# Wavelet attention in an eight-phase layer: the value products cut into four pieces, the result stored in five

## The chip, the cores and the metric

The kernel runs on one core of a Trainium2 chip. The metric is the device time of one execution in microseconds (us); lower is better. A core has five engines that run their own instruction streams and meet at semaphores: TensorE (PE in the profile, with its weight loads as PEld), VectorE (DVE), ScalarE (ACT), GpSimd (POOL) and SyncE (SP), which here only issues transfers (DMA).

## The reference

The input is `hidden_states`, 2 sequences of 2048 tokens with 128 channels, in f32. The kernel computes a chain of residual layers: a state-space (Mamba) block with a tanh block, a wavelet attention, a mixture of 8 experts, a sparse attention layer (4 of 16 heads), a layer with the diagonal of a softmax, and the sparse attention layer again. The change touches the wavelet attention and the end of the last layer. Cut to the wavelet attention and the last step:

```
xe, xo = x[:, 0::2], x[:, 1::2]
a, det = (xe + xo) * inv, (xe - xo) * inv          # 2 x 1024 x 128
q, k, v = (a @ w).reshape(B, 1024, 16, 8)           # 16 heads of 8 channels
att = softmax(einsum('bqhd,bkhd->bhqk', q, k) / sqrt(8))
o = einsum('bhqk,bkhd->bqhd', att, v) @ wo
...
return x + sparse_attention(layernorm(x))           # the last layer; its sum is the result
```

## The kernel before

The kernel is written engine by engine, with explicit semaphores. Each phase has one Python list of steps, and each engine walks it and emits its own part of every step, so the list sets the order on all engines. A `Signal` counts events; `T.wait_ge(*signal(event))` makes TensorE wait for one.

The wavelet attention is `phase_C`. It works in 8 rounds: 2 sequences times 4 groups of 4 heads. A round has 8 blocks of keys (`kt`, 128 keys each), and a block has 4 steps (`hh`, one head each), so 32 steps. The text calls these steps 0 to 31. A step is:

- E: `pe_exp` (L1432), two bf16 matmuls of 512 queries each, scores with the keys on the partitions, into a slot of two PSUM banks; ScalarE then takes the exponential of all 1024 (L1704) into one of the 8 buffers of `prob`.
- M: `pe_max` (L1420), two bf16 matmuls of the scores of the next round, queries on the partitions; VectorE reduces them to a row maximum (L1563). Steps 3, 10, 17 and 24 hold two of these, so that all 32 are made in steps 0 to 27. The last round has none.
- AV: `pe_av` (L1443), the product of the probabilities of the block before with the values (8 channels and a column of ones for the denominator). One call makes one half (512 queries) for 4 heads: f32 matmuls at `tile_position=(0, 32 * hh)`, so that the four heads share the array side by side. Each f32 matmul is two records in the profile, so a half is 8. The result accumulates in PSUM banks 6 and 7 over the 8 blocks of the round.

M and E share 3 PSUM slots in turn (`pe_slot`): a matmul waits until the user three places ahead of it has been read, by ScalarE after an E and by VectorE after an M. The halves of AV stand in front of E at `hh` 2 and 3 of the next block; the two halves of the last block stand in the step `fin` behind the round, after a wait for the last exponential. VectorE then copies banks 6 and 7 out (L1582). ScalarE waits, at the first head of a block, for the second half of the products that last read its buffer.

Two rounds carry more VectorE work than the others: the first has a layer norm beside it, the fifth (sequence 1, group 0) the convolution of sequence 0. The last round has transposes and routing for the next phase beside it.

The last layer is `phase_E("E2")`. Each tile of 128 tokens gets its last addition into `res` from L2480, which raises `summed` (`out_added`). After the phase `finish` waits for the drains of all engines (`enter(SP)`) and then stores all of `res` in one DMA of 2 MB.

Of the kernel before, what the change touches and what calls it, by code (L numbers as in the profile page):

```python
# [11 lines left out]
P = 128  # L12
D = 128
BANK = 512
# [85 lines left out]
def build(nc, a, out, shape, phases=("M", "C", "D", "E", "F", "E2")):  # L100
    NB, S, _ = shape
    NT = S // P
    R = NB * NT
    T, V, A, G, SP = nc.tensor, nc.vector, nc.scalar, nc.gpsimd, nc.sync
    ctx = ExitStack()
    with ctx:
# [1074 lines left out]
            return fd  # L1181

        routers = []

        def phase_C():
            routers.append(front_D())
# [5 lines left out]
            MR = NG * HD  # L1192
            INV = 0.7071067811865476
            SC = 1.0 / float(np.sqrt(HD))
            with ExitStack() as st:
                wqkv = sb(st, "w_qkv", [P, 3 * D])
                wo = sb(st, "w_o", [P, D])
# [110 lines left out]
                second_pass = signal("wl_shifted", at("exp"))  # L1308
                exped = signal("exp_done", at("exp"))
                quads = [(b, g, kt) for b, g in rounds_c for kt in range(CT)]  # L1310
                valued = signal("valued", [(*q, j) for q in quads for j in range(2)])
                oc_done = signal("out_copied", rounds_c)
                o_turned = signal("out_turned", pair("norm", 2))
                o_done = signal("wl_o_done", pair("norm", 2))
# [109 lines left out]
                def pe_exp(b, g, kt, hh):  # L1424
                    n = round_at[b, g]
                    if kt == 0:
                        T.wait_ge(*q_again(n, hh))
                    if kt and hh in (2, 3):
                        pe_av(b, g, kt - 1, hh - 2)
                    bk = pe_slot("exp", b, g, kt, hh)  # L1430
                    for j in range(2):
                        last = T.matmul(bank(bk + j), kT[n % 3][0:ROWS, hh, kt * P:(kt + 1) * P], qT[n % 3][0:ROWS, hh, j * BANK:(j + 1) * BANK], start=True, stop=True)  # L1432
                    last.then_inc(*second_pass.up(b, g, kt, hh))

                def pe_av(b, g, kt, j):

                    if j == 0:
                        T.wait_ge(*exped(b, g, kt, 3))
                        if kt == 0 and round_at[b, g]:
                            T.wait_ge(*oc_done(*rounds_c[round_at[b, g] - 1]))  # L1440
                    for hh in range(4):
                        n = unit_at[b, g, kt, hh] % 8
                        last = T.matmul(bank(6 + j)[32 * hh:32 * hh + HD + 1, :], vp[b][:, kt, 4 * g + hh, :],  # L1443
                                        prob[:, n, j * BANK:(j + 1) * BANK], start=(kt == 0), stop=(kt == CT - 1),
                                        skip_group_check=True, tile_position=(0, 32 * hh))
                    last.then_inc(*valued.up(b, g, kt, j))

# [31 lines left out]
                def pe():  # L1479
                    enter(T)  # L1480
                    for kind, *u in seq:
                        if kind == "turn":
                            pe_turn(*u)
                        elif kind == "qkv":
                            pe_qkv(*u)
                        elif kind == "max":
                            pe_max(*u)
                        elif kind == "exp":
                            pe_exp(*u)
                        elif kind == "fin":  # L1490
                            for half in range(2):
                                pe_av(*u, CT - 1, half)
                        elif kind == "norm":
                            pe_norm(*u)
                        elif kind == "co":
                            pe_co(*u)
                        elif kind == "wo":
                            pe_wo(*u)
                        elif kind == "yt":
                            pe_yt(*u)  # L1500
                        elif kind == "dch":
                            pe_dch(*u)
                        elif kind == "dlg":
                            fd.pe_logits(0, pe_slot("dlg"))
                        elif kind == "dgt":
                            fd.pe_gates(0, pe_slot("dgt"))
                    leave(T)
# [68 lines left out]
                    last.then_inc(*max_rows.up(b, g))  # L1576

                def dve_fin(b, g):
                    V.wait_ge(*valued(b, g, CT - 1, 1))
                    if round_at[b, g]:  # L1580
                        V.wait_ge(*o_turned(*rounds_c[round_at[b, g] - 1], 1))
                    V.tensor_copy(oc[:, :], two(6)).then_inc(*oc_done.up(b, g))  # L1582
# [116 lines left out]
                def act_exp(*u):  # L1699
                    A.wait_ge(*second_pass(*u))  # L1700
                    n = unit_at[u]
                    if n >= 8 and n % 4 == 0:
                        A.wait_ge(*valued(*quads[n // 4 - 2], 1))
                    A.activation(prob[:, n % 8, :], two(slot("exp", *u)), ACT.Exp, scale=SC).then_inc(*exped.up(*u))  # L1704

                def act():
# [491 lines left out]
        def phase_E(tag):  # L2198
# [4 lines left out]
            with ExitStack() as st:  # L2203
# [103 lines left out]
                def sp():  # L2307
                    enter(SP)
                    for b in range(NB):
# [2 lines left out]
                            fr.sp_heads(b)  # L2312
                        sp_swap(2 * b)
                    sp_swap(3)
                    leave(SP)

                def pe_piece(n, m, bk):
# [682 lines left out]
                pool()  # L3000

        def finish():
            enter(SP)
            store = loads("store")
            SP.dma_start(out.rearrange("b (i p) d -> p (b i) d", p=P), res[:, :, :]).then_inc(*store.one())
            SP.wait_ge(*store.all())

        run = {"M": phase_M, "C": phase_C, "D": phase_D, "E": lambda: phase_E("E"), "E2": lambda: phase_E("E2"), "F": phase_F}
# [24 lines left out]
```

## Time and profile before

| | us |
|---|---|
| three timed runs | 4373.02, 4373.57, 4366.19; median 4373.02 |
| profiled execution | 4358.43 |
| its span | 4357.1 |
| PE busy, share of the span | 3635.9 (83%) |
| DVE busy | 3294.0 (76%) |
| ACT busy | 2845.8 (65%) |
| POOL busy | 1001.8 (23%) |
| TensorE granted clock, mean | 0.823 |

The phases run one after the other; the wavelet rounds lie between about 636 and 1100 us from the span's start. In the chain that ended last, followed over the whole span, PE takes 41%, DVE 29%, "issue" 12% and ACT 6%. A record of a matmul lasts longer than the time after which the next can start, because matmuls are pipelined: the distance between the starts of two neighbours is what one costs. Each row of the timeline is start, duration, engine, line, operation, output and inputs, shape, count, and in brackets how long the engine was idle before it and who released it.

### The profile page before, as it was taken

The page shows a single profiled execution, that of the slowest core. Times are in us where ns is not written, and L with a number is a line of the kernel's source. Part 1 is how long each engine was busy: PE and PEld are TensorE (multiplying, and loading weights), DVE is VectorE, ACT ScalarE, POOL GpSimd, SP SyncE. Part 2 cuts the span into 40 slices and gives each one's busy share as a digit, 9 for nine tenths or more (in the row PEclk, how much of TensorE's full clock was granted, in tenths as well). Part 3 has the DMA queues.
Part 4 walks back from the last instruction along what each step waited for, and adds up shares of the span by engine and source line. Part 5 has one row for each costly group of instructions (what it writes and reads, how often), then busy time and mean ns, then how long its engine had stood idle before and what let it go on. Part 6 is the DMA issues. An engine that isn't in the chain of part 4 may idle for free.

```text
span 4357.1 us, 74462 instructions
## 1 busy us (share of the span) xinstructions
PE 3635.9 (83%) x28950; PEld 1917.7 (44%) x28950; DVE 3294.0 (76%) x5091; ACT 2845.8 (65%) x4856; POOL 1001.8 (23%) x1479
## 2 busy tenths in 40 slices
PE   6999868999799998999997666666666659899998
PEld 4666522222344445666665112222222215566776
DVE  6787767777311127887886999999999996778887
ACT  3655415556344445666664999999999995566665
POOL 2444432100467640000001232322332220000000
PEclk8999959999999999999998555555555559899999
DMA  1000032331511200000000111111110110000000
GB/s 48 1 1 1 1 69 38 54 58 20 114 26 37 39 17 9 12 7 12 2 2 16 22 22 22 22 22 22 22 19 19 22 20 21 7 12 7 7 2 21
DMA packets 256813, 97.51 MB, mean 22 GB/s; under 512 B 223795, under 2 KB 241854, under 8 KB 256446
## 3 DMA queue, kind: packets, MB, share of 16 engines
q1 hardware_dynamic: 256462, 92.74, 10.8%
q8 instruction: 231, 3.78, 0.4%
q14 instruction: 120, 0.98, 0.1%
HBM read 31.75 MB, written 2.23 MB: 8 GB/s over the span
## 4 chain that ended last, share of the span: by engine, by line
PE 41%; DVE 29%; issue 12%; ACT 6%; DMA 1%; POOL 0%; SPq 0%; DVEq 0%; ACTq 0%; POOLq 0%
DVE d_negmax L2825 14%; PE psum L2351 7%; PE psum L2380 6%; DVE f_m_E L2450 6%; PE psum L2366 6%; PE psum L2055 5%; PE psum L2077 5%; ACT d_junk L2883 3%; DVE wl_negmax L1563 3%; PE psum L1443 2%; PE psum L1432 2%; DVE f_pT_E L2469 2%; PE psum L1420 2%; ACT wl_p L1704 1%; DVE residual L2480 1%
## 5 line engine op out<-in xcount | busy, mean ns | idle before, releaser
L2825 DVE TENSOR_REDUCE d_negmax<-psum 128x1 f32<-128x1024 f32 x1024 | 1170.9, 1210 | 25.4 <-PE psum L2761 23.4
L2883 ACT ACTIVATE d_junk<-psum,d_negmax 128x1024 bf16<-128x1024 f32 x1024 | 1136.0, 1125 | 37.1 <-DVE d_negmax L2825 32.6
L2761 PE MATMUL psum<-d_qT,d_kT 64*128 64x512 bf16 x2048 | 622.9, 604 | 432.1 <-ACT d_junk L2883 414.9
L2544 ACT ACTIVATE hidden<-psum,f_nm_E 128x1024 f32<-128x1024 f32 x512 | 566.0, 1112 | 143.5 <-DVE f_nm_E L2453 143.4
L2450 DVE TENSOR_REDUCE f_m_E<-psum 128x1 f32<-128x1024 f32 x512 | 601.6, 1216 | 46.8 <-PE psum L2351 45.6
L2351 PE MATMUL psum<-f_k_E,f_q_swapped_E 64*128 64x512 f32 x1024 | 526.9, 624 | 6.6 <-ACT hidden L2544 6.6
L2351 PE MATMUL psum<-f_k_E,f_q_E 64*128 64x512 f32 x1024 | 526.6, 624 | 2.9 <-DVE f_v_E L2441 1.9
L2551 ACT COPY f_pT_E<-psum 128x512 f32<-128x512 f32 x512 | 299.4, 585 | 322.3 <-PE psum L2366 322.3
L2380 PE MATMUL psum<-f_pT_E,f_v_E 128*64 128x128 f32 x8192 | 505.0, 276 | 2.5 <-DVE residual L2480 2.5
L2761 PEld LDWEIGHTS psum<-d_qT,d_kT 64*128 64x128 bf16 x2048 | 107.9, 101 | 842.9 <-ACT d_junk L2883 761.1
L2469 DVE COPY f_pT_E<-psum 128x512 f32<-128x512 f32 x512 | 351.3, 686 | 159.5 <-PE psum L2366 150.0
L2380 PEld LDWEIGHTS psum<-f_pT_E,f_v_E 128*64 128x64 f32 x8192 | 443.6, 137 | 20.0 <-ACT f_pT_E L2551 2.8
L2366 PEld LDWEIGHTS psum<-ident,hidden 64*128 64x128 f32 x8192 | 317.9, 140 | 238.2 <-issue 189.1
L1704 ACT ACTIVATE wl_p<-psum 128x1024 f32<-128x1024 f32 x256 | 255.4, 1023 | 240.3 <-PE psum L1432 239.0
L2366 PE MATMUL psum<-ident,hidden 64*128 64x64 f32 x8192 | 358.6, 227 | 50.7 <-DVE f_pT_E L2469 47.1
L2189 POOL TENSOR_TENSOR moe_h<-moe_h,moe_gates_on_all 128x512 f32<-128x512 f32 x256 | 322.3, 1291 | 320.9 <-DMA moe_gates_on_all<-moe_gate_spill 187.5
L1563 DVE TENSOR_REDUCE wl_negmax<-psum 128x1 f32<-128x1024 f32 x256 | 303.7, 1219 | 77.7 <-PE psum L1420 74.9
L2167 ACT ACTIVATE moe_h<-psum,moe_b 128x512 f32<-128x512 f32 x256 | 174.8, 687 | 254.7 <-PE psum L2077 254.6
L2055 PE MATMUL psum<-moe_h,moe_w 128*128 128x512 f32 x512 | 231.6, 594 | 1.8 <-POOL moe_h L2189 1.5
L2883 ACT ACTIVATION_READ_ACCUMULATOR d_junk<-psum,d_negmax 128x1 f32 x1024 | 214.4, 209 | 0.0
L2077 PE MATMUL psum<-normed_channels,moe_w 128*128 128x512 f32 x448 | 205.0, 601 | 4.9 <-DMA moe_w<-in_moe_w 4.9
L2351 PEld LDWEIGHTS psum<-f_k_E,f_q_E 64*128 64x128 f32 x1024 | 160.5, 189 | 92.9 <-ACT hidden L2544 79.2
(331 smaller groups left out, 4736.3 us busy)
## 6 DMA issues: line engine op xcount, KB each, us to landing
moe_gates_on_all<-moe_gate_spill SPq DMA_DIRECT2D x16, 1024.0 KB, 11.9
f_q_swapped_E<-f_q_E SPq DMA_DIRECT2D x64, 128.0 KB, 2.3
moe_w<-in_moe_w SPq DMA_DIRECT2D x15, 256.0 KB, 6.5
out<-residual SPq DMA_DIRECT2D x1, 2048.0 KB, 8.7
residual<-in_hidden_states SPq DMA_DIRECT2D x2, 768.0 KB, 7.3
wl_qT<-wl_q_rows SPq DMA_TRANSPOSE x48, 3.3
residual<-in_hidden_states SPq DMA_DIRECT2D x2, 256.0 KB, 3.5
m_taps<-in_m_conv SPq DMA_DIRECT2D x4, 128.0 KB
```

Source lines behind the costliest of these rows:

```text
L1563: V.tensor_reduce(negm[:, i, h:h + 1], two(slot("max", b, h, i)), X, ALU.max, negate=True).then_inc(*maxed.up(b, h, i))
L2055: last = T.matmul(acc, w2[:, e * FT + f, :], hbuf[:, n % 2, f, :], start=False, stop=(e == E_ - 1 and f == FT - 1))
L2077: T.matmul(bank(f), w1(e)[:, f * P:(f + 1) * P], chans[:, b, PAD + g * BANK:PAD + (g + 1) * BANK], start=True, stop=True).then_inc(*made.u ...
L2351: last = T.matmul(bank(2 * f + jj), (q if jj == h else q_sw)[half, w, qs], k2[half, w, h, f, :], start=True, stop=True)
L2366: last = T.transpose(bank(4 + r)[:, q * 64:(q + 1) * 64], pb[half, u % 2, kt * P:(kt + 1) * P], ident[half, half])
L2380: last = T.matmul(bank(6)[64 * h:64 * h + 64, 0:P], vt[:, n % 2, kt, h, :], pT[:, (2 * t + h) % 4, kt, :], start=(kt == 0), stop=(kt == NT ...
L2450: last = V.tensor_reduce(m2[:, u % 4, f:f + 1], two(2 * f), X, ALU.max)
L2469: V.tensor_copy(pT[:, u % 4, 8 * g:8 * g + 8, 64:P], bank(5).rearrange("p (q n) -> p q n", n=64)).then_inc(*pT_dve.up(u, g))
L2544: A.activation(pb[:, u % 2, f * 2 * BANK:(f + 1) * 2 * BANK], two(2 * f), ACT.Exp, bias=nm[:, u % 4:u % 4 + 1], scale=SC, accum_out=rs[:, ...
L2761: last = T.matmul(bank(2 + 2 * (at % 3) + jj), kT[half, s, jb * P:(jb + 1) * P], qT[half, s, hf * BANK:(hf + 1) * BANK], start=True, stop= ...
L2825: V.tensor_reduce(mh[:, t % 2, n // 2, n % 2:n % 2 + 1], two(2 + 2 * (at % 3)), X, ALU.max, negate=True).then_inc(*maxed.up(at))
L2883: A.activation(junk[:, at % 3, :], two(2 + 2 * (at % 3)), ACT.Exp, bias=mh[:, t % 2, n // 2, n % 2:n % 2 + 1], accum_out=sh[:, t % 2, n // ...
```

## The change

Two parts. In `phase_C`, an AV call now makes a quarter (256 queries, `AV = 4` pieces of a block), and one piece stands in front of each E: pieces 0 to 2 of the block before at `hh` 1 to 3, and piece 3 of the block before that at `hh` 0. `fin` has five pieces, the last of block 6 and the four of block 7. The waits for `valued` name the last piece. At the end, the one store in `finish` becomes five, issued by SP inside `E2`, each behind the addition of its last tile: 16 tiles (all of sequence 0), 8, 4, 3 and 1.

```diff
+            AV = 4
...
-                    if kt and hh in (2, 3):
-                        pe_av(b, g, kt - 1, hh - 2)
+                    if hh and kt:
+                        pe_av(b, g, kt - 1, hh - 1)
+                    if hh == 0 and kt >= 2:
+                        pe_av(b, g, kt - 2, AV - 1)
                     bk = pe_slot("exp", b, g, kt, hh)
...
+                    size = 2 * BANK // AV
+                    at = j * size % BANK
                     for hh in range(4):
                         n = unit_at[b, g, kt, hh] % 8
-                        last = T.matmul(bank(6 + j)[32 * hh:32 * hh + HD + 1, :], vp[b][:, kt, 4 * g + hh, :],
-                                        prob[:, n, j * BANK:(j + 1) * BANK], start=(kt == 0), stop=(kt == CT - 1),
+                        last = T.matmul(bank(6 + j * size // BANK)[32 * hh:32 * hh + HD + 1, at:at + size], vp[b][:, kt, 4 * g + hh, :],
+                                        prob[:, n, j * size:(j + 1) * size], start=(kt == 0 and at == 0), stop=(kt == CT - 1),
                                         skip_group_check=True, tile_position=(0, 32 * hh))
...
-                            for half in range(2):
-                                pe_av(*u, CT - 1, half)
+                            pe_av(*u, CT - 2, AV - 1)
+                            for j in range(AV):
+                                pe_av(*u, CT - 1, j)
...
-                        A.wait_ge(*valued(*quads[n // 4 - 2], 1))
+                        A.wait_ge(*valued(*quads[n // 4 - 2], AV - 1))
...
+        stored = [(0, NT), (NT, NT + NT // 2), (NT + NT // 2, R - 4), (R - 4, R - 1), (R - 1, R)]
...
+                    if tag == "E2":
+                        for lo, hi in stored:
+                            b, i = (hi - 1) // NT, (hi - 1) % NT
+                            SP.wait_ge(*summed(((b * NPAIR + NPAIR - 1) * NT + i), 1))
+                            SP.dma_start(out_rows[:, lo:hi, :], res[:, lo:hi, :]).then_inc(*store.one())
...
         def finish():
-            enter(SP)
-            store = loads("store")
-            SP.dma_start(out.rearrange("b (i p) d -> p (b i) d", p=P), res[:, :, :]).then_inc(*store.one())
             SP.wait_ge(*store.all())
```

On TensorE, the fourth round (sequence 0, group 3), steps 18 to 21, before. L1443 is AV, L1432 is E, L1420 is M; x4 counts the matmuls of the program, one a head.

```order
L1443 MATMUL psum<-wl_p,wl_v 9x512 x4
L1432 MATMUL psum<-wl_qT,wl_kT 128x512 x2
L1420 MATMUL psum<-wl_kT,wl_qT 128x512 x2
L1443 MATMUL psum<-wl_p,wl_v 9x512 x4
L1432 MATMUL psum<-wl_qT,wl_kT 128x512 x2
L1420 MATMUL psum<-wl_kT,wl_qT 128x512 x2
L1432 MATMUL psum<-wl_qT,wl_kT 128x512 x2
L1420 MATMUL psum<-wl_kT,wl_qT 128x512 x2
L1432 MATMUL psum<-wl_qT,wl_kT 128x512 x2
L1420 MATMUL psum<-wl_kT,wl_qT 128x512 x2
L1443 MATMUL psum<-wl_p,wl_v 9x512 x4
```

The same steps in the changed kernel, where AV is L1451, E is L1438 and M is L1424.

```order
L1451 MATMUL psum<-wl_p,wl_v 9x256 x4
L1438 MATMUL psum<-wl_qT,wl_kT 128x512 x2
L1424 MATMUL psum<-wl_kT,wl_qT 128x512 x2
L1451 MATMUL psum<-wl_p,wl_v 9x256 x4
L1438 MATMUL psum<-wl_qT,wl_kT 128x512 x2
L1424 MATMUL psum<-wl_kT,wl_qT 128x512 x2
L1451 MATMUL psum<-wl_p,wl_v 9x256 x4
L1438 MATMUL psum<-wl_qT,wl_kT 128x512 x2
L1424 MATMUL psum<-wl_kT,wl_qT 128x512 x2
L1451 MATMUL psum<-wl_p,wl_v 9x256 x4
L1438 MATMUL psum<-wl_qT,wl_kT 128x512 x2
L1424 MATMUL psum<-wl_kT,wl_qT 128x512 x2
```

Two halves in front of two of the four E have become four quarters, one in front of each.

On TensorE, the end of the same round before, from the last M to the first E of the next round:

```order
L1420 MATMUL psum<-wl_kT,wl_qT 128x512 x2
L1432 MATMUL psum<-wl_qT,wl_kT 128x512 x4
L1443 MATMUL psum<-wl_p,wl_v 9x512 x4
L1432 MATMUL psum<-wl_qT,wl_kT 128x512 x2
L1443 MATMUL psum<-wl_p,wl_v 9x512 x4
L1432 MATMUL psum<-wl_qT,wl_kT 128x512 x2
L1443 MATMUL psum<-wl_p,wl_v 9x512 x8
L1432 MATMUL psum<-wl_qT,wl_kT 128x512 x2
```

and in the changed kernel:

```order
L1424 MATMUL psum<-wl_kT,wl_qT 128x512 x2
L1451 MATMUL psum<-wl_p,wl_v 9x256 x4
L1438 MATMUL psum<-wl_qT,wl_kT 128x512 x2
L1451 MATMUL psum<-wl_p,wl_v 9x256 x4
L1438 MATMUL psum<-wl_qT,wl_kT 128x512 x2
L1451 MATMUL psum<-wl_p,wl_v 9x256 x4
L1438 MATMUL psum<-wl_qT,wl_kT 128x512 x2
L1451 MATMUL psum<-wl_p,wl_v 9x256 x4
L1438 MATMUL psum<-wl_qT,wl_kT 128x512 x2
L1451 MATMUL psum<-wl_p,wl_v 9x256 x20
L1438 MATMUL psum<-wl_qT,wl_kT 128x512 x2
```

There is a piece in front of each of the last four E, and 20 matmuls of 256 in place of 8 of 512 behind the last; the first four of the 20 belong to the block before and do not wait for the last exponential.

On SP, the end of the program before, from the last swaps of queries (L2303 and L2304) to the store:

```order
L2303 DMA f_q_swapped_E<-f_q_E 64x512 [waits ffn_qk_done]
L2304 DMA f_q_swapped_E<-f_q_E 64x512
L2303 DMA f_q_swapped_E<-f_q_E 64x512 [waits ffn_qk_done]
L2304 DMA f_q_swapped_E<-f_q_E 64x512
L3005 DMA out<-residual 128x32x128 [waits phase_end_act,phase_end_pool,phase_end_dve,phase_end_pe]
```

and in the changed kernel:

```order
L2312 DMA f_q_swapped_E<-f_q_E 64x512 [waits ffn_qk_done]
L2313 DMA f_q_swapped_E<-f_q_E 64x512
L2328 DMA out<-residual 128x16x128 [waits out_added]
L2328 DMA out<-residual 128x8x128 [waits out_added]
L2328 DMA out<-residual 128x4x128 [waits out_added]
L2328 DMA out<-residual 128x3x128 [waits out_added]
L2328 DMA out<-residual 128x128 [waits out_added]
```

The stores stand behind the last swap and wait for additions, no longer for the drains of the four other engines.

## Rows read from the trace of the kernel before

**Rows 1.** Windows, four wavelet rounds: stretch, busy us, clock, DMA share, GB/s.
```profile
758.94:820.28 61.34, 55.06 (x265) 14.39 (x266) 42.22 (x49) 32.09 (x32) 8.69 (x26) 0.89 0.33 62
820.28:875.82 55.54, 51.01 (x265) 13.27 (x264) 41.94 (x49) 31.99 (x32) 6.52 (x19) 0.97 0.34 57
875.82:942.53 66.71, 60.18 (x293) 16.09 (x292) 55.73 (x64) 32.90 (x33) 6.52 (x19) 0.90 0.32 54
...
1052.77:1099.66 46.89, 42.81 (x249) 14.13 (x247) 22.95 (x64) 34.87 (x38) 0.00 (x0) 0.89 0.06 11
```
**Rows 2.** Timeline, steps 18 to 21 of the fourth round.
```profile
851.10 1.04 PE L1443 MATMUL psum<-wl_p,wl_v 128*9 128x512 f32 x8
...
852.08 0.61 PE L1432 MATMUL psum<-wl_qT,wl_kT 75*128 75x512 bf16 x2
...
852.52 0.59 PE L1420 MATMUL psum<-wl_kT,wl_qT 75*128 75x512 bf16 x2
...
853.05 1.05 PE L1443 MATMUL psum<-wl_p,wl_v 128*9 128x512 f32 x8
...
854.03 0.60 PE L1432 MATMUL psum<-wl_qT,wl_kT 75*128 75x512 bf16 x2
...
854.47 0.59 PE L1420 MATMUL psum<-wl_kT,wl_qT 75*128 75x512 bf16 x2
854.67 1.94 ACT L1704 ACTIVATE wl_p<-psum 128x1024 f32<-128x1024 f32 x2 [0.92 <-PE psum L1432]
...
854.90 0.59 PE L1432 MATMUL psum<-wl_qT,wl_kT 75*128 75x512 bf16 x2
855.10 3.64 DVE L1563 TENSOR_REDUCE wl_negmax<-psum 128x1 f32<-128x1024 f32 x3 [0.72 <-PE psum L1420]
...
855.75 0.60 PE L1420 MATMUL psum<-wl_kT,wl_qT 75*128 75x512 bf16 x2 [0.25 <-ACT wl_p L1704]
...
856.38 0.60 PE L1432 MATMUL psum<-wl_qT,wl_kT 75*128 75x512 bf16 x2
...
856.83 0.59 PE L1420 MATMUL psum<-wl_kT,wl_qT 75*128 75x512 bf16 x2
...
857.35 1.04 PE L1443 MATMUL psum<-wl_p,wl_v 128*9 128x512 f32 x8
```
**Rows 3.** Timeline of PE, the fourth round: first AV, step 26 to the end.
```profile
831.03 1.04 PE L1443 MATMUL psum<-wl_p,wl_v 128*9 128x512 f32 x8
...
864.46 1.05 PE L1443 MATMUL psum<-wl_p,wl_v 128*9 128x512 f32 x8
...
867.38 0.61 PE L1432 MATMUL psum<-wl_qT,wl_kT 75*128 75x512 bf16 x2
...
872.13 0.60 PE L1432 MATMUL psum<-wl_qT,wl_kT 75*128 75x512 bf16 x2
873.85 1.90 PE L1443 MATMUL psum<-wl_p,wl_v 128*9 128x512 f32 x16 [1.11 <-ACT wl_p L1704]
875.68 0.60 PE L1432 MATMUL psum<-wl_qT,wl_kT 75*128 75x512 bf16 x2
```
**Rows 4.** Timeline of PE, last round: one block of four steps.
```profile
1065.97 1.05 PE L1443 MATMUL psum<-wl_p,wl_v 128*9 128x512 f32 x8 [0.25 <-ACT wl_p L1704]
...
1070.18 1.05 PE L1443 MATMUL psum<-wl_p,wl_v 128*9 128x512 f32 x8 [0.25 <-ACT wl_p L1704]
```
**Rows 5.** Timeline, the end: last addition and the store's issue.
```profile
4347.52 0.74 DVE L2480 SCALAR_TENSOR_TENSOR residual<-psum,f_rs_E,residual 128x128 f32<-128x128 f32 x2 [0.35 <-PE psum L2394]
4348.38 0.41 SPq L3005 DMA_DIRECT2D out<-residual  x1
```
**Rows 6.** DMA view: issue, KB each, us from issue to landing (windows and whole).
```profile
out<-residual SPq DMA_DIRECT2D x1, 2048.0 KB, 8.7
...
moe_gate_spill<-moe_gate_rows SPq DMA_DIRECT2D x1, 64.0 KB, 1.6
...
f_q_swapped_E<-f_q_E SPq DMA_DIRECT2D x64, 128.0 KB, 2.3
```

More of the change, by code:

```diff
@@ L1183, in build @@
         routers = []
+        store = loads("store")
+        out_rows = out.rearrange("b (i p) d -> p (b i) d", p=P)
+        stored = [(0, NT), (NT, NT + NT // 2), (NT + NT // 2, R - 4), (R - 4, R - 1), (R - 1, R)]
         def phase_C():
@@ L1310, in phase_C @@
                 quads = [(b, g, kt) for b, g in rounds_c for kt in range(CT)]
-                valued = signal("valued", [(*q, j) for q in quads for j in range(2)])
+                valued = signal("valued", [(*q, j) for q in quads for j in range(AV)])
                 oc_done = signal("out_copied", rounds_c)
@@ L1578, in dve_fin @@
                 def dve_fin(b, g):
-                    V.wait_ge(*valued(b, g, CT - 1, 1))
+                    V.wait_ge(*valued(b, g, CT - 1, AV - 1))
                     if round_at[b, g]:
```

## The prediction, made before the changed kernel was timed

> **What bounds the kernel now.** I read the windows by round first [rows 1]; they are cut where VectorE copies the result of a round out. A round in the middle takes 55.54 us. PE is busy for 51.01 of it, DVE for 41.94 and ACT for 31.99, so no engine is full and PE is nearest. Next I read the timeline of one block of four steps [rows 2], since a share says nothing on where the waits fall. It shows two kinds of steps. In the first two a half of AV stands in front of E, and PE is the last to be ready: AV at 851.10, E 852.08, M 852.52, next AV 853.05, which is 1.95 us a step. In the last two there is no AV, and PE waits: M at 855.75 was queued behind E at 854.90 and waited for ScalarE to empty a slot (E at 854.03, exponential from 854.67, free for PE at 855.75, 1.72 after E), and E at 856.38 for VectorE (M at 854.47, reduction from 855.10, free 1.91 after M). So PE's work is uneven: too much in two steps, too little in two, with three slots that carry nothing over. Third, the end of a round [rows 3] and of the program [rows 5, 6].
>
> **Price of a piece.** E to M to E costs PE 0.43 to 0.44 (854.03, 854.47, 854.90 in [rows 2]). M to AV costs 0.53 (852.52 to 853.05), so entering AV costs 0.10 more than entering scores. AV to E costs 0.98 (853.05 to 854.03). Two halves back to back and then E cost 1.83 (873.85 to 875.68 in [rows 3]), so a half streams for 1.83 - 0.98 = 0.85 and leaving AV costs 0.98 - 0.85 = 0.13. A visit to AV has a fixed price of 0.23, which a quarter pays as well. No row has a quarter. From below it streams for half of 0.85, and AV to E is 0.98 - 0.43 = 0.55; from above it is as long as a half, 0.98. I take 0.55: in the rows a half is a stream whose length is the number of queries, and the fixed part has been taken out already.
>
> The row shows PE losing 0.10 on the way in and 0.13 on the way out. The Trainium skill (TensorEngine Tiling (Array Packing), section Tiling Modes, Key Properties) says that changing the tiling mode, not just the tile, drains TensorE. By that rule the fixed price is no accident of these rows, and each further visit costs it again; the trace agrees with 0.23.
>
> **A block after.** Each step is AV 0.55, E 0.44, M 0.53: 1.52 us, and a block of four is 6.08. Do waits remain? M needs the E of the step before plus 1.72, and stands at 1.52 + 0.44 = 1.96. E needs the M two steps back plus 1.91 and stands at 0.53 + 0.55 + 0.44 + 0.53 + 0.55 = 2.60. The first piece of a block needs the last exponential of the block before, about 1.72 after its E, and stands 2.49 after it. A reduction is 1.21 (three in 3.64) and fits into 1.52. All have room, so PE becomes the bound, with no wait. ScalarE's wait for its buffer names a piece that PE does just ahead of the E which the same exponential waits for, so nothing queues behind it. Before, the block took 857.35 - 851.10 = 6.25, so a plain block wins only 0.17: 0.62 of waits goes, 2 visits x 0.23 = 0.46 comes. A block with a second M in a step took 864.46 - 857.35 = 7.11 and becomes 6.08 + 0.43 = 6.51; the reductions then queue for up to 0.12, so 6.51 to 6.63.
>
> **A round after.** From the first AV of the fourth round to its E of step 27 were 867.38 - 831.03 = 36.35 us [rows 3]. After, from the piece of step 6: 21 steps x 1.52 = 31.92, three second M at 0.43 to 0.55 (1.3 to 1.65), and the last piece to E 0.55: 33.8 to 34.1. I take 2.4 us of gain. It is more than the blocks alone give because the twelve halves there (24 quarters) are 22 quarters now: one quarter goes ahead, into step 5, where PE stands waiting for VectorE, and one behind, into the wait for the last exponential (1.11 us of idle time at 873.85). From E of step 27 to that AV were 6.47 (867.38 to 873.85). After: 1.52 to step 28, three steps of 0.53 + 0.55, and the same 1.72 from the last E (872.13) to AV: 6.48, no change. The four pieces behind it stream as long as the two halves.
>
> Over the eight rounds: five like this one, 5 x 2.4 = 12.0. The first and the fifth carry other VectorE work; in the fifth, 875.82 to 942.53 in [rows 1], DVE is busy for 55.73 of 66.71. There PE hardly sets the pace: 0 to 2.4 each, I take 0.7, together 1.4. The last has no M, so the visits are all that changes: a block took 1070.18 - 1065.97 = 4.21 [rows 4]; after it is 4 x (0.53 + 0.55) = 4.32, and the first piece of a block, 1.61 after the E that it needs, waits for the remaining 0.11: 4.43. Seven blocks lose up to 1.5; I take 1.2. Sum: 12.0 + 1.4 - 1.2 = 12.2 us.
>
> **The store.** The last addition ends at 4348.26, the store issues at 4348.38 [rows 5] and lands 8.7 later [rows 6], at the end of the span. After, four of the five stores (31 of 32 tiles) have gone before: the fourth can issue when the last tile but one is added, and one tile of attention takes several us more. Alone behind the last addition is a store of 64 KB. The bounds from [rows 6]: 1.6 us (64 KB to memory, with a free queue) and 2.3 (128 KB inside the core). I take 1.8, so 6.9 us of gain (6.4 to 7.1). SP has nothing else to do after its last swap, so the early stores hold nothing up, and the additions that they wait for are final.
>
> On a write of 64 KB the row shows 1.6. The Trainium skill (DMA: Bandwidth & Descriptors, the table of the fixed cost) gives about 2.0 us of fixed cost, most of it the receipt of the write; by that the estimate for this term would be 8.7 - 2.0 = 6.7.
>
> **Sum.** 12.2 + 6.9 = 19.1 us. The profiled execution took 4358.4 and becomes 4339.3. It is 14.6 below the median of the three timed runs, 4373.0, for which no row gives a reason; I take the difference over to the median: 4353.9.
>
> **Rivals.**
> 1. A quarter costs more than 0.55, or another wait takes over. The gain in the rounds hangs on some 170 quarters at which PE sets the pace (5 x 22, the last round's 28, some 30 in the two others), so each 0.01 us more costs 1.7 us, and at 0.62 the rounds win nothing. For it: no row has a quarter, and eight matmuls and eight weight loads now have half the time to be fed. Against it: the scores next to it feed at 0.22 a matmul, and this would be 8 in 0.43, no more than one matmul each 0.05. The store's gain remains: 4373.0 - 6.9 = 4366.1.
> 2. The clock. The third round (758.94 to 820.28) took 61.34 at a granted clock of 0.89, the fourth 55.54 at 0.97 [rows 1], with the same work: a part of the third ran at the lower level, 1.2 GHz of 2.4. Work for PE is now more even. If the lower level goes from the third round and from half of the other rounds' share, I estimate 5.8 + 3 = 8 us more gain: 4346. It can also come the other way by as much; the starts of rounds themselves change by one quarter only, which speaks against both.
> 3. The other side: PE is the bound already, and what looks like waits between the steps comes back elsewhere, at the slots. Then only the new visits count. A round had 15 (14 halves and the pair at the end) and has 28: 13 x 8 = 104 more, at 0.23 each 24 us lost. With the store, 24 - 6.9 = 17 slower: 4390. This is what the tiling page's rule gives when nothing else moves. It decides once the waits that go and the quarters that find idle time are worth less than those 24 us; in my sum they are worth 36. Against it: 0.62 of waits in a plain block, with room of 0.24 and 0.69 at the two slots after.
>
> **Chances.** Forecast 0.67; rival 1, only the store's gain, 0.17; rival 2, 0.10; rival 3, 0.04; the remaining 0.02 is a loss of the clock or on another phase. A measurement of this kernel can tell about 0.2% from no change, 8.7 us, so faster means below 4364.3. The forecast and rival 2 lie there nearly whole (0.74), and rival 1, whose mean is 4366, with two fifths of its chance (0.06): faster 0.80, same 0.15, slower 0.05. The forecast's own range is 4346 to 4362: its terms' bounds (11 to 14 for the rounds less 3 for the first and fifth, 6.4 to 7.1) and 5 for the scatter of 7 us between the timed runs. Toward the rivals I widen to 4343 and 4368.
>
> **What would show it.** In the timeline of a middle round: pieces of AV of 8 records with 0.55 to the next E, no wait of PE for DVE or ACT between steps 6 and 27, 1.52 us a step; windows by round near 53 us for the second, fourth, sixth and seventh and 1 us more for the last; ScalarE's exponentials evenly spaced; the last store landing under 2.3 us after its issue. I would be wrong if AV to E costs 0.65 or more, if M still waits for ScalarE in the middle of a round, or if the clock row by round differs by more than 0.05 from that of before.

## The result, and the profile after

The changed kernel takes 4383.35 us (median of 10 runs, 4376.22 to 4388.72); the kernel before took 4370.00 in the same comparison (10 runs, 4363.74 to 4374.58). The ratio is 1.003, 95% interval 1.002 to 1.004: slower by 13 us, where I forecast 19 us faster. The profiled execution took 4379.18 with a span of 4377.9, against 4358.43 and 4357.1.

First the windows by round of the changed kernel, cut at the same copies as in [rows 1], now over all eight rounds (the first stretch begins ahead of the round). Columns: stretch, its length, then busy us of PE, PEld, DVE, ACT and POOL with their counts, granted clock, DMA share, GB/s.

```profile
582.00:723.64 141.64, 120.19 (x449) 23.21 (x450) 91.99 (x141) 37.33 (x38) 30.88 (x64) 0.52 0.31 60
723.64:782.85 59.21, 57.21 (x424) 18.85 (x422) 48.29 (x52) 38.45 (x50) 21.25 (x21) 1.00 0.22 37
782.85:842.57 59.72, 55.53 (x393) 16.48 (x394) 42.43 (x50) 32.78 (x32) 9.24 (x27) 0.89 0.34 65
842.57:894.34 51.77, 50.13 (x393) 14.29 (x392) 42.15 (x49) 32.67 (x32) 6.55 (x19) 1.00 0.36 62
894.34:959.22 64.88, 59.55 (x421) 18.78 (x420) 55.75 (x65) 33.26 (x33) 7.31 (x22) 0.92 0.32 55
959.22:1010.98 51.76, 50.12 (x393) 14.31 (x392) 42.14 (x49) 32.66 (x32) 2.63 (x8) 1.00 0.32 54
1010.98:1062.81 51.83, 50.19 (x393) 14.30 (x392) 45.16 (x66) 32.68 (x32) 0.00 (x0) 1.00 0.11 22
1062.81:1119.32 56.51, 54.28 (x377) 16.11 (x375) 23.10 (x64) 36.38 (x38) 0.00 (x0) 0.73 0.04 9
```

The third, fourth, fifth and last of these rounds answer to the four of [rows 1]. The fourth went from 55.54 to 51.77 us, and the six rounds in the middle together from 356.1 (1052.77 - 696.69) to 339.2 us (1062.81 - 723.64): 16.9 us of gain. But the first round ends at 723.64, where it ended at 696.69 before, 27.0 us later, and the last takes 56.51 in place of 46.89 in [rows 1]. In exactly these two the granted clock is low, 0.52 and 0.73. In the kernel before, the same two stretches had 0.72 (582.00 to 696.69) and 0.89: the difference of more than 0.05 in a round that I had named as a sign of being wrong. The sum at the end of the rounds is 1119.32 - 1099.66 = 19.7 us lost.

Next, the first round cut where the clock changes, before:

```profile
636.00:650.10 14.10, 14.01 (x37) 3.49 (x38) 9.90 (x15) 6.14 (x6) 3.38 (x10) 0.50 0.62 118
650.10:696.69 46.59, 40.52 (x222) 9.28 (x221) 37.57 (x74) 28.52 (x29) 3.14 (x9) 1.00 0.20 38
```

and the same of the changed kernel, with the late part of the last round:

```profile
635.70:722.40 86.70, 86.56 (x368) 18.09 (x372) 48.69 (x88) 35.55 (x35) 6.61 (x20) 0.50 0.23 44
...
1091.10:1118.40 27.30, 27.16 (x153) 4.74 (x156) 8.79 (x15) 12.49 (x13) 0.00 (x0) 0.50 0.01 3
```

Before, the low level (0.50, which is 1.2 of 2.4 GHz) ends 14 us into the round. In the changed kernel it goes on for 86.70 us, the rest of the round, and again for 27.30 us in the last. What to see is PE's busy time beside it: 86.56 of 86.70 us. TensorE was idle for 0.14 us there, and the clock stayed down all the same.

### The profile page after: what moved, and what is told of

It is laid out like the page before. It is cut to its first block, busy times and chain, and to the rows that moved or that the text cites. A ratio compares the mean times of both kernels' runs of the same rounds, so it can differ in the third digit from the quotient of the medians.

```text
span 4377.9 us, 76512 instructions
## 1 busy us (share of the span) xinstructions
PE 3685.8 (84%) x29974; PEld 1939.8 (44%) x29974; DVE 3296.7 (75%) x5091; ACT 2853.9 (65%) x4856; POOL 1003.9 (23%) x1479
## 4 chain that ended last, share of the span: by engine, by line
PE 44%; DVE 28%; issue 11%; ACT 5%; DMA 1%; POOL 0%; SPq 0%; DVEq 0%; ACTq 0%; POOLq 0%
DVE d_negmax L2839 14%; PE psum L2365 7%; PE psum L2394 6%; DVE f_m_E L2464 6%; PE psum L2380 6%; PE psum L2086 5%; PE psum L2064 5%; ACT d_junk L2897 3%; PE psum L1451 3%; PE psum L1438 3%; PE psum L1424 2%; DVE f_pT_E L2483 2%; DVE wl_negmax L1572 2%; DVE residual L2494 1%; PE psum L2338 1%
```

## The experiments

The theory after the comparison: at the low level single quarters, with scores between them, do not bring the clock back, while a half does. The rival: the new steps, or something behind the rounds, cost more than I took. All kernels below have the value products placed by a list `PLAN` with one entry a round, and unless said otherwise the store in five pieces:

```
QUARTERS = (4, lambda kt: [(1, 1), (1, 2), (1, 3), (2, 0)])   # pieces; (blocks later, hh) of each
HALVES   = (2, lambda kt: [(1, 2), (1, 3)])
```

Medians stand beside those of the kernel before on the same chip. The length of the rounds is from each kernel's trace, first / middle six together / last, where the first is counted from ScalarE's first record of the exponential's line, which lies ahead of the round; by that count before is 113.8 / 356.1 / 46.9 and the change 141.1 / 339.2 / 56.5.

**1. Store only.**

```diff
-PLAN = [QUARTERS] * 8
+PLAN = [HALVES] * 8
```

> The kernel before with only the store changed (five pieces), the value products in halves as before. Both theories expect the store's gain alone: 6.4 to 7.1 us less than before (4370 becomes about 4363), and the last store landing within 2.3 us of its issue. If the store does less than 3 us here, my term for it was wrong.

Measured: 4361.26 against 4369.18, ratio 0.9982 (0.9972 to 0.9991), 8 us. Rounds 118.6 / 356.3 / 46.8; the last store landed 1.5 us after its issue. The store's term holds. The low level in the first round ended at 667 us here, not at 650, and so it did in experiments 3 and 5 (668). PE's timeline has three halves (L1469) at the low level ahead of that:

```profile
652.62 1.90 PE L1469 MATMUL psum<-wl_p,wl_v 128*9 128x512 f32 x8
...
656.27 1.90 PE L1469 MATMUL psum<-wl_p,wl_v 128*9 128x512 f32 x8
...
663.33 1.90 PE L1469 MATMUL psum<-wl_p,wl_v 128*9 128x512 f32 x8
```

Behind the first two nothing rose. So a half does not end the low level each time; one of the first three did in every profiled first round with halves. What decides which one is not shown.

**2. Value products only**, the store as before.

> Only the value products in quarters, one store as before. Theory A (the clock): the quarters take away what raised TensorE's clock from 1.2 to 2.4 GHz in the first round (before: up at 650 us, after: up at 722 us) and hold it low in the last (27 us), so this is slower than before by 13 + 7 = 20 us, about 4390, and the middle rounds 1 to 6 are 16 us shorter together. Theory B (the steps themselves cost more, or what follows the wavelet rounds is what lengthened): the loss is not in the first and last round; the middle rounds win less than 10 us.

Measured: 4388.63 against 4369.18, 1.0044 (1.0031 to 1.0057). Rounds 141.5 / 339.4 / 56.5: the loss is in the first and the last round, the gain in the six between.

**3. Halves at both ends.**

```diff
-PLAN = [QUARTERS] * 8
+PLAN = [HALVES] + [QUARTERS] * 6 + [HALVES]
```

> Quarters in rounds two to seven, halves in the first and in the last, and the store in five. Theory A: the clock is up at about 650 us again as in the kernel before, the last round is back at 47 us, and the middle rounds keep their 16 us: 16 + 7 = 23 us faster than before, about 4347. Theory B: about as slow as the changed kernel, or at best the store's 7 us (4363).

Measured: 4350.66 against 4369.18, 0.9954 (0.9941 to 0.9967). Rounds 118.5 / 341.6 / 45.1. The quarters' gain stands once the two rounds are spared.

**4. Quarters in the first round alone**, `PLAN = [QUARTERS] + [HALVES] * 7`.

> Quarters in the first round alone, halves in the other seven, the store in five. Theory A: the first round alone costs 25 to 28 us by the clock, so 27 - 7 = 20 us slower than before, about 4390, and its clock rises only where the pieces stand back to back, at the end of the first round. Theory B (not the clock): one round cannot cost more than 3 us, about 4365.

Measured: 4393.05 against 4369.18, 1.0055 (1.0042 to 1.0068). Rounds 141.2 / 357.2 / 46.9. One eighth of the change alone costs more than all of it.

**5. Quarters in pairs.**

```diff
-QUARTERS = (4, lambda kt: [(1, 1), (1, 2), (1, 3), (2, 0)])
+PAIRS = (4, lambda kt: [(1, 2), (1, 2), (1, 3), (1, 3)])
```

> All eight rounds in pieces of 256 as in the change, but two of them back to back where a half stood (in front of hh 2 and of hh 3), the store in five. If it is the placing of the pieces one by one that keeps the clock low, the clock rises at 650 to 667 us as with halves, the rounds are as long as before (62, 61, 56, 67, 56, 54, 47) and the time is that of the store alone, 4361. If it is the size of a matmul (256 columns in place of 512), the first round stays at 141 us and the time is near 4390.

Measured: 4363.25 against 4368.62, 0.9979 (0.997 to 0.9988). Rounds 118.6 / 356.6 / 47.3: like halves in every respect. The matmul's size is not it; how many products stand together is.

**6. Four quarters together once**, in block 0 of the first round:

```diff
+QUARTERS_FIRST_TOGETHER = (4, lambda kt: [(1, 1)] * 4 if kt == 0 else [(1, 1), (1, 2), (1, 3), (2, 0)])
+PLAN = [QUARTERS_FIRST_TOGETHER] + [QUARTERS] * 7
```

> The changed kernel with one difference: in the first round the four quarters of block 0 stand back to back in front of one E (step 5); all later pieces one by one. If the low clock is a state that one streak of products ends and single quarters then do not bring back, the clock rises within some us of that streak (about 650 us), the first round falls from 141 to about 116 us, and the time is 25 us under the changed kernel, near 4358; the last round stays at 56. If single quarters cannot hold the clock in the first round either, it falls back and the gain is under 8 us (4376).

Measured: 4370.49 against 4368.62, 1.0016 (0.9996 to 1.0035), rounds 133.8 / 342.2 / 54.9. Of its 12 executions one took 4416.92. The first round is 7.3 us shorter than in the change, where I expected 25, and by the ratios (1.0016 against 1.003) the whole gain is 6 us: the second branch of the expectation. The windows of its first round, cut where the clock changes:

```profile
632.00:649.40 17.40, 11.62 (x46) 3.45 (x50) 11.03 (x21) 5.12 (x5) 3.39 (x10) 0.50 0.48 92
649.40:666.60 17.20, 14.36 (x104) 3.87 (x96) 14.48 (x35) 11.46 (x12) 3.16 (x9) 1.00 0.48 92
666.60:717.80 51.20, 50.48 (x238) 10.23 (x242) 25.01 (x39) 18.75 (x19) 1.24 (x4) 0.50 0.11 21
```

and PE's timeline where it fell (L1444 is M, L1456 E, L1469 AV):

```profile
647.27 2.98 PE L1469 MATMUL psum<-wl_p,wl_v 128*9 128x256 f32 x32
...
665.09 0.61 PE L1456 MATMUL psum<-wl_qT,wl_kT 75*128 75x512 bf16 x2
667.18 1.01 PE L1444 MATMUL psum<-wl_kT,wl_qT 75*128 75x512 bf16 x2 [1.49 <-ACT wl_p L1730]
668.12 1.04 PE L1469 MATMUL psum<-wl_p,wl_v 128*9 128x256 f32 x8
```

The streak at 647.27 did bring the clock up, at 649.40. The clock fell again at 666.60, while PE waited 1.49 us for ScalarE, and then stayed down for 51.20 us with PE busy for 50.48. Single quarters held the high level until PE waited, and did not restore it after. Shorter waits ahead of this one, of up to 0.61 us, did not end it.

**7. Halves further apart in the first round**, at `hh` 1 and 3 in place of 2 and 3, `PLAN = [(2, lambda kt: [(1, 1), (1, 3)])] + [HALVES] * 7`.

> Halves in all rounds, but in the first they stand in front of hh 1 and hh 3, with two E and two M between them in place of one each; the store in five. If it is how closely the products follow each other that raises the clock, it rises later than 667 us or not before the end of the round, and the time is up to 25 us over that of the store alone (4361 to 4386). If it is the length of a half, nothing changes: 4361.

Measured: 4360.30 against 4368.62, 0.9975 (0.9964 to 0.9987), rounds 114.9 / 356.6 / 47.0. The clock rose at 650.6, fell at 667.7, behind a wait of PE of 1.63 us for ScalarE, and was back 3.4 us later. Both times one half stood ahead of the rise with E and M around it, so two halves close together are not needed. My expectation of a loss was wrong, the one that a single half does it right, though experiment 1 shows that it does not do it each time.

**8. One streak in the first round, halves in the last**, `PLAN = [QUARTERS_FIRST_TOGETHER] + [QUARTERS] * 6 + [HALVES]`.

> As the last but one (four quarters together once in the first round), quarters one by one in rounds two to seven, halves in the last round, the store in five. By the clock theory it has the gains of all and the losses of none: 4348 to 4351, like the kernel with halves in the whole first round, or 2 us better, since the first round's quarters win a little. If single quarters fail in the first round, it is 10 us or more slower than that.

Measured: 4367.31 against 4368.62, 0.9997 (0.9988 to 1.0006), rounds 134.1 / 339.5 / 48.1. A miss, for the reason seen in 6: one streak is not enough. The clock fell again at 670.2, in the same wait of 1.49 us. The second branch held: it is 17 us slower than experiment 3 (4350.66 on another chip; 19 us by the ratios).

**9. Added products.** The changed kernel with a second, discarded computation of the first quarter of each block in the first and last round:

```diff
                     bk = pe_slot("exp", b, g, kt, hh)
+                    if n in PADDED and kt and hh == 1:        # PADDED = (0, 7)
+                        for q in range(4):
+                            T.matmul(bank(bk)[32 * q:32 * q + HD + 1, 0:256], vp[b][:, kt - 1, 4 * g + q, :],
+                                     prob[:, unit_at[b, g, kt - 1, q] % 8, 0:256], start=True, stop=True,
+                                     skip_group_check=True, tile_position=(0, 32 * q))
```

> The changed kernel with work added: in the first and the last round, once a block, the first quarter of the products is computed a second time into the slot that the next E overwrites, right behind the real one, so that two quarters' worth of products stand together (7 blocks x 2 rounds, 0.43 us each at the high level of the clock, 6 us in all). If the loss is the clock and a longer stretch of products is what ends its low level, the added work makes the kernel faster: the first round falls from 141 to 117 or so, the last from 56 to 48, and the time from 4383 to 4353 to 4360. If the loss is TensorE's own work in these rounds, it is 6 us slower than the changed kernel, 4389.

Measured: 4343.23 against 4368.93, 0.9939 (0.9926 to 0.9953), rounds 113.5 / 342.2 / 50.4. Work that is thrown away makes the kernel 40 us faster than the change, by the times and by the ratios alike. PE's timeline in the first round (L1477 is AV, L1460 the added products, L1464 E, L1447 M):

```profile
646.35 1.04 PE L1477 MATMUL psum<-wl_p,wl_v 128*9 128x256 f32 x8
647.16 1.08 PE L1460 MATMUL psum<-wl_p,wl_v 128*9 128x256 f32 x8
648.18 0.77 PE L1464 MATMUL psum<-wl_qT,wl_kT 75*128 75x512 bf16 x2
648.79 0.59 PE L1447 MATMUL psum<-wl_kT,wl_qT 75*128 75x512 bf16 x2
```

The two quarters at 646.35 and 647.16 stand together, the E at 648.18 is already shorter, and from the M at 648.79 the matmuls run at the high level; the windows on both sides of it:

```profile
636.00:648.50 12.50, 11.65 (x39) 3.25 (x40) 8.71 (x14) 5.12 (x5) 3.38 (x10) 0.50 0.56 108
648.50:697.10 48.60, 46.00 (x403) 12.89 (x402) 38.87 (x74) 30.33 (x30) 3.14 (x9) 1.00 0.25 48
```

**10. Quarters in the last round alone**, `PLAN = [HALVES] * 7 + [QUARTERS]`.

> Quarters in the last round alone, halves in the other seven, the store in five. By the clock theory the clock falls behind the long run of transposes for the routing, in the second half of the round, as it does for 3.4 us with halves, and then stays at 1.2 GHz to the five pieces at the end: the last round takes 55 to 57 us in place of 47, and the time is 9 us over that of the store alone, 4370. If each visit's fixed price were all, it would be 1.2 to 1.5 us: 4363.

Measured: 4375.97 against 4368.93, 1.0013 (1.0004 to 1.0023), 15 us over the store alone (on another chip; 14 us by the ratios). One of its ten executions took 6723.53 us and is outside the ratio; why is not known. The loss is more than expected, and the profiled execution (4363.57, the fastest of the ten) does not show it: there the last round took 49.1 us, and the low level behind the routing products lasted 6.9 us and ended at 1097.0 with nothing but single quarters and E since the fall. So in the last round, which has no M between the pieces, single quarters can bring the level back. The mean granted clock of the eight others of ordinary length is 0.818 to 0.820, against 0.822 of the profiled one. Time at the low level counts half in the mean, so 0.003 less is some 26 us more of it, an estimate from these means, which do not say where in the kernel it was. Where the other 6 us are I cannot tell from the one trace.

**11. Added scores.** As 9, of the same length, but the two bf16 matmuls of E twice:

```diff
-                        for q in range(4):
-                            T.matmul(bank(bk)[32 * q:32 * q + HD + 1, 0:256], ...
+                        for j in range(2):
+                            T.matmul(bank(bk + j), kT[n % 3][0:ROWS, hh, kt * P:(kt + 1) * P], ...
```

> The changed kernel with work added as in the padded one, in the same places and of the same length (0.43 us at the high level), but of the other kind: the two bf16 matmuls of E are done twice, once a block, in the first and the last round. If it is only that TensorE must be given more work, this is as fast as the padded kernel, 4343. If it is the stretch of value products that counts (TensorE was already busy for 50.48 of 51.20 us while the clock stayed low), the clock stays at 1.2 GHz through the first round, 141 us and more, and the time is 4383 to 4397.

Measured: 4391.65 against 4374.65, 1.0042 (1.0028 to 1.0055), rounds 147.5 / 345.1 / 55.4. The same amount of TensorE time in the same places, and the first round stays low to its end:

```profile
636.00:723.00 87.00, 85.60 (x338) 19.04 (x338) 48.69 (x88) 32.48 (x32) 6.52 (x19) 0.50 0.18 35
```

Busy for 85.60 of 87.00 us, clock 0.50. The amount of work alone does not do it; the same length of value products did.

**12. Added products in the first round, halves in the last**, `PLAN = [QUARTERS] * 7 + [HALVES]`, `PADDED = (0,)`.

> The best of the parts: quarters one by one in rounds one to seven, the added products in the first round alone, halves in the last round, the store in five. The last round took 50.4 us with added products and 45.1 to 48.1 with halves, so this should be 2 to 5 us under the padded kernel: 4338 to 4343. If it is above 4345, halves in the last round give nothing more.

Measured: 4347.57 against 4374.65, 0.9939 (0.9926 to 0.9953), rounds 113.5 / 342.2 / 45.3. The time lies over the expected 4338 to 4343, on a chip where the kernel before is 6 us slower as well. The last round is 5 us shorter than in 9, but the ratio is the same; the two are not to be told apart. Both beat the kernel before and the change by 0.6% and 0.9%.

## Why the prediction was wrong

**The price of a piece and of a block: right.** PE's timeline in the fourth round of the changed kernel, rows that answer to [rows 2] and [rows 3]: the piece of step 6, one step in the middle, and the piece and E of step 27 (L1451 is AV, L1438 E, L1424 M):

```profile
852.05 0.62 PE L1451 MATMUL psum<-wl_p,wl_v 128*9 128x256 f32 x8
...
863.14 0.62 PE L1451 MATMUL psum<-wl_p,wl_v 128*9 128x256 f32 x8
863.69 0.60 PE L1438 MATMUL psum<-wl_qT,wl_kT 75*128 75x512 bf16 x2
864.13 0.59 PE L1424 MATMUL psum<-wl_kT,wl_qT 75*128 75x512 bf16 x2
864.66 0.62 PE L1451 MATMUL psum<-wl_p,wl_v 128*9 128x256 f32 x8
...
885.30 0.62 PE L1451 MATMUL psum<-wl_p,wl_v 128*9 128x256 f32 x8
885.86 0.61 PE L1438 MATMUL psum<-wl_qT,wl_kT 75*128 75x512 bf16 x2
```

AV to E is 0.55, E to M 0.44, M to AV 0.53, the step 1.52, all as worked out, and no wait of PE for DVE or ACT is left between step 6 and step 27. From the piece of step 6 to E of step 27 are 33.81 us, in the middle of the 33.8 to 34.1, against 36.35 before: 2.5 us of gain, for which I took 2.4. The rival that charged each new visit and removed nothing is out: 78 more visits stand in the six middle rounds, and they are 16.9 us shorter.

**The middle rounds: right for the steps, with luck in the sum.** I had 5 x 2.4 for the five middle rounds other than the fifth and 0.7 for the fifth, 12.7 us; the trace has 16.9. The windows of before that [rows 1] does not show, the second, the sixth and the seventh round:

```profile
696.69:758.94 62.25, 57.84 (x296) 18.10 (x294) 48.08 (x51) 37.47 (x50) 22.84 (x25) 0.97 0.22 41
...
942.53:998.44 55.91, 52.14 (x265) 13.56 (x264) 42.03 (x49) 31.98 (x32) 3.38 (x10) 0.94 0.28 50
998.44:1052.77 54.33, 49.62 (x265) 12.28 (x264) 44.97 (x65) 31.99 (x32) 0.00 (x0) 1.00 0.13 20
```

The seventh round has a clock of 1.00 before and after and won 2.5 us, the term as worked out; the third has 0.89 both times and won 1.6. The second, fourth and sixth won 3.0, 3.8 and 4.2, and in just these a short stretch at 1.2 GHz (3.4, 3.4 and 6.8 us) is there before and gone after. In the fourth the parts can be told: 2.5 in steps 6 to 27, and 1.3 ahead of the piece of step 6, where that stretch was (827.5 to 830.9) and where a quarter now stands between the scores of step 5. Over the six rounds the time at the low level fell from 40.8 to 23.8 us. So a part of the 16.9, at most half of those 17 us by an estimate, is the clock's, which the sum did not count. It is rival 2 come true in a small way, though not in the third round, where I looked for it.

**The store: right.** 8.7 to 1.5 us, 7.2 in place of 6.9. The other estimate of the prediction, with 2.0 us for the last store, was 0.5 short. The rows that answer to [rows 5] and [rows 6], of the changed kernel, the end first and then the last store:

```profile
4375.54 0.74 DVE L2494 SCALAR_TENSOR_TENSOR residual<-psum,f_rs_E,residual 128x128 f32<-128x128 f32 x2 [0.35 <-PE psum L2408]
4376.30 0.34 SPq L2328 DMA_DIRECT2D out<-residual  x1
```
```profile
out<-residual SPq DMA_DIRECT2D x1, 64.0 KB, 1.5
```

**The first and the last round: the step that failed.** It is the sentence "The first and the fifth carry other VectorE work ... I take 0.7" and, for the last round, "the visits are all that changes". Both took the prices of the rows, which are prices at the high level, into rounds of which a part ran at 1.2 GHz, gave the clock no term in the sum, and assumed that the clock would change where it had changed before. Instead of 0.7 gained and 1.2 lost, the two lost 27.0 and 9.6 us. In the chapter on the clock I wrote that the starts of rounds "change by one quarter only, which speaks against both": I looked at where the clock was low, not at what had ended it. The trace of before had that, ahead of the rise at 650.1:

```profile
645.64 1.03 PE L1432 MATMUL psum<-wl_qT,wl_kT 75*128 75x512 bf16 x2
646.46 1.06 PE L1420 MATMUL psum<-wl_kT,wl_qT 75*128 75x512 bf16 x2
647.45 1.90 PE L1443 MATMUL psum<-wl_p,wl_v 128*9 128x512 f32 x8
649.28 0.95 PE L1432 MATMUL psum<-wl_qT,wl_kT 75*128 75x512 bf16 x2
650.07 0.60 PE L1420 MATMUL psum<-wl_kT,wl_qT 75*128 75x512 bf16 x2
```

PE ran E and M back to back at the low level (their starts mostly 0.82 to 0.87 apart, twice the 0.43 of the high level) from 636 on and nothing came of it; then came the first half, 8 records and 1.83 us without a break, and the next E was already shortening. The change cuts just this. In its first round the same place is

```profile
653.56 1.04 PE L1451 MATMUL psum<-wl_p,wl_v 128*9 128x256 f32 x8
654.54 1.03 PE L1438 MATMUL psum<-wl_qT,wl_kT 75*128 75x512 bf16 x2
655.37 1.06 PE L1424 MATMUL psum<-wl_kT,wl_qT 75*128 75x512 bf16 x2
656.36 1.04 PE L1451 MATMUL psum<-wl_p,wl_v 128*9 128x256 f32 x8
```

with single quarters from 645.18 on, for over 70 us, until the five pieces at the end of the round, which do stand together:

```profile
719.75 3.81 PE L1451 MATMUL psum<-wl_p,wl_v 128*9 128x256 f32 x40
723.49 0.61 PE L1438 MATMUL psum<-wl_qT,wl_kT 75*128 75x512 bf16 x2
```

E behind them, at 723.49, is fast. Experiments 4, 5, 6, 9 and 11 show each link against the store alone: single quarters in this round make it 22.6 us longer (141.2 against 118.6), two of them together cost nothing, a streak lifts the clock once, products added lift it within the first block in both kernels that have them (9 and 12), and scores added do not.

**Why the middle rounds were spared.** The clock falls in them as well, in the third (787.3 to 800.9) behind a wait of PE of 3.37 us for a transfer, and in the fifth (944.3 to 954.5) behind one of 1.80 us for VectorE. In the changed kernel's third round, PE's timeline ahead of the recovery (L1462 is the eight f32 transposes of the output):

```profile
797.96 1.91 PE L1462 MATMUL psum<-ident,wl_oT 128*128 128x128 f32 x8
799.80 1.04 PE L1451 MATMUL psum<-wl_p,wl_v 128*9 128x256 f32 x8
800.78 0.67 PE L1438 MATMUL psum<-residual 75*128 75x512 bf16 x2
```

The transposes and the piece behind them follow each other without scores between them, and E at 800.78 runs at nearly the high level. In the fifth round the level came back at 954.5, within eight other f32 transposes (L1484, from 953.23) that follow four single pieces with E alone between them. The first round has no transposes: PE does only E, M and AV there. Its clock fell in experiments 6 and 7 where PE waits for ScalarE. In the last round the fall needs no wait. It comes at 1091.10, at the end of 32 short products for the routing, which the expectation of experiment 10 calls transposes:

```profile
1087.85 3.90 PE L1122 MATMUL psum<-moe_wg,normed_channels 128*128 128x8 f32 x32
```

Behind it single quarters and E follow, with one transpose among them, and the level stays low for 27.30 us, to the five pieces; in experiment 9, with the added quarter, it was back after 6.8 us. Before, with halves, it was low for 3.4 us there. This reading of the middle rounds was not tested by an experiment of its own.

**The rest.** The two profiled spans differ by 20.8 us: 27.0 - 16.9 + 9.6 = 19.7 in the rounds, and 1.1 behind and before them, in which the store's 7.2 us of gain are contained. So some 8 us more went to the phases behind. From the last round's copy to the end of the span, the kernels with the new store had 3251.1 to 3256.9 us in the other traces and 3258.6 here; before, less the store's gain, it would be 3250.3. The clock goes with it: in the first 150 us behind the rounds it is 0.90 here and in experiments 3 and 5 (3256.9 and 3256.4), 0.92 in experiment 7 (3256.8), and 0.94 before and in experiments 1 and 8 (3252.6 and 3253.4). The phases behind are the same in all of them, so I take it for scatter of the clock; no experiment tests it.

The terms of the traces with the store add up to -7.2 + 27.0 - 16.9 + 9.6 = 12.5 us, near the 13 us between the timed medians. The timed experiments do not add up as well. Against the store alone, the first round costs 32 us (4393.05 against 4361.26, same chip), quarters in the middle win 11 (4350.66, same chip) and the last round costs 14 to 15; with -8 for the store that is 27 to 28, twice what the whole change costs. The signs agree with the traces, the sizes hold to some 15 us, and why is open.

In the forecast the clock had a tenth of the chance and a price of 8 us either way. It should have had a price worked out beforehand: a round wholly at the low level. The scores had a row at that level, 0.85 in place of 0.43, and a step in the changed kernel took 2.80 us there (653.56 to 656.36) in place of 1.52. With such a term the range reaches 30 us to the slow side.

## What to carry to other kernels

Before work on TensorE is cut finer or spread, look in the trace for the places where the granted clock rises and note what TensorE did just ahead; a change that removes this can cost more in one stage than it wins in all others, as here 27.0 us against 16.9. An engine that is busy all the time is no sign that the clock is high: prices taken from rows hold for the level of those rows only. Where a stage starts at the low level, keep the unbroken stretch of matmuls that stood ahead of the rise, even at the price of added work, and spread the pieces only where the trace shows that the level is high and comes back after a fall.

## What the runs showed of the hardware

- TensorE at 1.2 GHz for 86.70 us while busy for 86.56 of them, with steps of two bf16 score pairs of 75 rows and one f32 piece of 8 records. The same steps ran at 2.4 GHz in most of the six middle rounds (clock 0.89 to 1.00).
- What came just ahead of a rise: 8 f32 records of 512 columns (1.83 us at the low level), 16 of 256 (experiments 5 and 9), 40 of 256, or 8 f32 transposes and a piece. What did not bring one: over 70 us of pieces of 8 records of 256 between pairs of scores, and added bf16 scores (experiment 11). In the last round of experiment 10, pieces of 8 records with E alone between them were followed by a rise after 6.9 us; in the changed kernel they were not in 27.30 us. Two halves of 1.83 us in experiment 1 passed without one.
- What came just ahead of a fall, in the places read: waits of TensorE of 1.49 to 3.37 us; in the fourth round before, some 7 us of nothing but scores with waits of at most 0.52 us (820.15 to 827.5); or 32 f32 products of 8 columns (3.90 us) with no wait.
- Work that is thrown away, 14 x 0.43 us, won 40 us (4343.23 against 4383.35, on different chips; by the ratios to the kernel before, 0.9939 and 1.003).
- Entering and leaving the four column tiles costs 0.23 us at the high level, the same for a quarter as for a half (AV to E 0.55 and 0.98, M to AV 0.53 for both).
- A store of 64 KB landed 1.5 to 1.6 us after its issue.
